# Score and maxima banks regrouped in the self and cross attention steps of a three-attention transformer block

## What is computed

```python
def _attn(x, ctx, wq, wk, wv, wo, bo, heads):       # heads = 20, dh = 16
    q, k, v = (x @ wq), (ctx @ wk), (ctx @ wv)      # split into heads
    sim = jnp.einsum('bhid,bhjd->bhij', q, k) * scale
    a = jax.nn.softmax(sim, axis=-1)
    out = jnp.einsum('bhij,bhjd->bhid', a, v)
    return out @ wo + bo
x = _attn(h1, h1, q1, k1, v1, o1_w, o1_b, heads) + x          # self, 512 keys
x = _attn(h2, context, q2, k2, v2, o2_w, o2_b, heads) + x     # cross, 1024 keys
```

## Time and profile before

| | us |
|---|---|
| median of 3 runs | 851.36 |
| the profiled execution | 850.15 |
| its span in the profile | 848.4 |
| self steps with maxima | 343.33 to 435.08 |
| self tail | to 448.7 |
| cross lead | 482 to 497 |
| first cross values | 501.64 |
| cross steps with maxima | to 690.7 |
| cross tail | to 713.1 |

### The profile page before, as it was taken

How to read it: one execution, slowest core, us unless ns; L and a number is a source line. 1 busy time by engine, 2 the same in 40 slices (tenths; PEclk the granted TensorE clock), 3 DMA queues, 4 the chain that set the end, 5 groups by cost and what they waited for, 6 DMA issues and landing times.

```text
span 848.4 us, 11644 instructions
## 1 busy us (share of the span) xinstructions
PE 802.2 (95%) x4178; PEld 442.8 (52%) x4178; DVE 584.4 (69%) x1102; ACT 488.7 (58%) x748; POOL 127.5 (15%) x209
## 2 busy tenths in 40 slices
PE   4889999999999999999999889999999999999998
PEld 3777644444466675333335543333333333678888
DVE  4354668777584648899956579999999962693241
ACT  4543544445553552776777767767677678862130
POOL 5000103100005241100014500000000002640000
PEclk9998999999999999999999969999999999999999
DMA  8887577532302066222135502232222120200000
GB/s 288 272 272 216 166 221 250 161 100 64 112 19 71 3 216 189 77 76 76 40 61 90 190 12 57 58 57 54 45 50 62 39 73 40 78 1 1 32 0 32
DMA packets 31255, 83.18 MB, mean 98 GB/s; under 512 B 5205, under 2 KB 9245, under 8 KB 28639
## 3 DMA queue, kind: packets, MB, share of 16 engines
q1 hardware_dynamic: 30398, 79.71, 32.6%
q0 software_dynamic: 800, 2.73, 1.0%
HBM read 56.12 MB, written 25.89 MB: 97 GB/s over the span
## 4 chain that ended last, share of the span: by engine, by line
PE 70%; DVE 15%; DMA 6%; ACT 4%; issue 4%; SPq 1%; POOL 0%; ACTq 0%; DVEq 0%; POOLq 0%
PE PS L1016 20%; PE PS L959 15%; PE PS L633 8%; PE PS L996 7%; PE PS L1647 7%; DVE maxp L1163 5%; PE PS L1665 4%; DMA k_d<-split 3%; DVE negm L1163 3%; PE PS L1468 3%; ACT probs L1123 2%; DVE turned L1208 1%; DMA w_v<-in_Wv 1%; ACT act_t L1541 1%; DMA q_sl<-msplit 1%
## 5 line engine op out<-in xcount | busy, mean ns | idle before, releaser
L1123 ACT ACTIVATE probs<-PS 128x1024 f32<-128x1024 f32 (+1 forms) x336 | 310.6, 972 | 138.4 <-PE PS L996 135.4
L1163 DVE TENSOR_REDUCE maxp<-PS 128x1 f32<-128x512 f32 (+1 forms) x400 | 251.7, 679 | 41.0 <-PE PS L959 40.0
L959 PE MATMUL PS<-k_sl,q_sl 48*128 48x512 f32 (+2 forms) x592 | 221.2, 446 | 8.7 <-DVE maxp L1163 2.1
L996 PE MATMUL PS<-q_sl,k_sl 50*128 50x512 f32 (+3 forms) x672 | 201.1, 428 | 4.2 <-ACT probs L1123 2.7
L959 PEld LDWEIGHTS PS<-k_sl,q_sl 48*128 48x128 f32 (+2 forms) x592 | 101.1, 186 | 163.5 <-DVE maxp L1163 105.3
L1163 DVE TENSOR_REDUCE negm<-PS 128x1 f32<-128x512 f32 (+1 forms) x192 | 121.6, 678 | 20.9 <-PE PS L959 20.1
L996 PEld LDWEIGHTS PS<-q_sl,k_sl 50*128 50x128 f32 (+2 forms) x672 | 101.3, 189 | 49.4 <-ACT probs L1123 21.1
L1016 PE MATMUL PS<-probs,v2c 128*32 128x512 f32 x640 | 87.4, 616 | 1.0
L675 DVE TENSOR_TENSOR split<-PS,split 128x512 fp32r<-128x512 f32 (+3 forms) x54 | 34.8, 649 | 52.4 <-ACT split L650 52.1
L1016 PE MATMUL PS<-probs,v0c 128*64 128x512 f32 (+1 forms) x256 | 62.0, 605 | 0.0
L650 ACT CAST split<-PS 128x512 fp32r<-128x512 f32 (+3 forms) x54 | 29.9, 555 | 50.2 <-PE PS L633 32.4
(11 more groups left out here) (203 smaller groups left out, 1092.9 us busy)
## 6 DMA issues: line engine op xcount, KB each, us to landing
k_d<-split SPq DMA_DIRECT2D x20, 512.0 KB, 3.9
q_d<-split SPq DMA_DIRECT2D x12, 512.0 KB, 4.0
k_sl<-k_d SPq DMA_DIRECT2D x8, 640.0 KB
k_sl<-k_d SPq DMA_DIRECT2D x40, 128.0 KB, 5.6
q_sl<-q_d SPq DMA_DIRECT2D x40, 128.0 KB
k_sl<-k_d SPq DMA_DIRECT2D x20, 256.0 KB, 5.4
w_raw<-in_ff_w SPq DMA_DIRECT2D x3, 1280.0 KB, 6.9
k_sl<-k_d SPq DMA_DIRECT2D x8, 320.0 KB
```

The lines of the kernel that those rows point to most:

```text
L959: nc.tensor.matmul(PS[0:a.qt, SBANKS[k % 3], 0:cn], q_view(g)[f:f + a.rows, j // a.stack, q * a.qt:(q + 1) * a.qt], k_view(g)[f:f + a.rows ...
L996: mm = nc.tensor.matmul(PS[0:sz, 2 * (x % 2) + half, 0:a.nq], k_view(g)[f:f + a.rows + 2, j // a.stack, t * 128:t * 128 + sz], q_view(g)[f ...
L1123: nc.scalar.activation(probs[0:a.size[t], x % PRING, :, 0:a.nq], PS[0:a.size[t], 2 * (x % 2):2 * (x % 2) + 2, 0:a.nq], ACT.Exp, scale=a.sc ...
L1163: nc.vector.tensor_reduce((maxp if nch > 1 else negm)[0:a.qt, g.turn, o:o + 1], PS[0:a.qt, SBANKS[k % 3], 0:a.chunks[c][1]], AX.X, ALU.max ...
```

## The change

In the self and cross streams (`st.single`) scores use single banks: 0, 1 and 2 in turn, and each head has an exponential of its own, 128 x 512, with a count of its own (`st.exp` starts at 3, `st.pair` counts scores). Bank 3 joins 4, 5 and 6 for the items and flips of the steps, the least recently used first. In the tails, from two steps after the last maxima (`st.tail`), scores may use banks 3 to 6 also, less the one that the last flip has. `bank_uses` and `score_banks` write down for each use its bank and the use before it. TensorE's order in a step becomes two items, two scores, two items, two scores, the values, the flips. The filler products go from 4 and 2 to 3 and 2. The first stream keeps pairs and three maxima banks. SyncE's waits on `st.pair` count scores in place of pairs (`scored_to`).

```diff
+def bank_uses(st):
+    st.bank, st.before = {}, {}
+    last, order = {}, [3] + list(SBANKS)
+    def take(ring, k, by):
+        b = next(n for n in order if n in ring)
+        st.bank[k], st.before[k], last[b] = b, last.get(b), by
+        order.remove(b)
+        order.append(b)
...
+        ring = (3,) + SBANKS if st.single and c >= st.lead else SBANKS
...
+def score_banks(st):
+    st.sbank, st.sbefore, last = {}, {}, {}
+    order = [0, 1, 2] + [b for b in (3,) + SBANKS if b != st.bank[st.flip_use[len(st.groups) - 1]]]
+    st.tail = len(st.steps) - st.lead + 2
+    for y in range(2 * st.all_pairs):
+        b = next(n for n in order if n < 3 or y >= 4 * st.tail)
+        st.sbank[y], st.sbefore[y], last[b] = b, last.get(b), y
+        order.remove(b)
+        order.append(b)
...
+        def score(i, t, j):
...
+            y = 2 * st.first_pair[i] + t * a.g + j
+            if st.sbefore[y] is not None:
+                pe.wait_ge(st.exp, 3 + st.sbefore[y] + 1)
+            elif y >= 3:
+                pe.wait_ge(st.score_free, st.all_items)
+            f = a.base(j)
+            nc.tensor.matmul(PS[:, st.sbank[y], 0:a.nq], ...).then_inc(st.pair, 1)
...
-            pe.wait_ge(st.exp, x + 3)
+            pe.wait_ge(st.exp, 2 * x + 5 if st.single else x + 3)
...
             for s in range(len(st.steps)):
-                if st is S_SELF and s == 0:
-                    keep_busy(4)
-                if s + 1 < len(st.steps):
-                    scores(*st.steps[s + 1], 0)
-                maxima(st.chunks_at(s), 0, 2)
+                more = s + 1 < len(st.steps)
                 if st is S_SELF and s == 0:
                     keep_busy(2)
-                if s + 1 < len(st.steps):
-                    scores(*st.steps[s + 1], 1)
+                maxima(st.chunks_at(s), 0, 1)
+                maxima(st.chunks_at(s), 1, 2)
+                if more:
+                    score(*st.steps[s + 1], 0)
+                if more:
+                    score(*st.steps[s + 1], 1)
                 maxima(st.chunks_at(s), 2, 3)
+                maxima(st.chunks_at(s), 3, 4)
+                if more:
+                    score(*st.steps[s + 1], 2)
+                if more:
+                    score(*st.steps[s + 1], 3)
                 for p in range(2):
                     values(*st.steps[s], p)
-                maxima(st.chunks_at(s), 3)
                 flips(st.chunks_at(s))
...
                 act.wait_ge(st.used, x + 1)
+                if st.single:
+                    for half in range(2):
+                        act.wait_ge(st.pair, 2 * x + half + 1)
+                        nc.scalar.activation(probs[:, x % PRING, half, 0:a.nq], PS[:, st.sbank[2 * x + half], 0:a.nq],
+                                             ACT.Exp, scale=a.scale).then_inc(st.exp, 1)
+                    x += 1
+                    continue
```

More of the change, by code:

```diff
@@ L97, in __init__ @@
         self.name = name
+        self.single = name != "first"
         self.groups = []
@@ L121, in __init__ @@
             self.negated_to.append(negated)
-        self.all_pairs = pairs
+        self.all_pairs, self.all_items = pairs, items
         self.lead = self.groups[0].a.lead
@@ L127, in pairs_to, with scored_to @@
         return self.first_pair[i] + self.groups[i].a.kt * self.groups[i].a.pairs
+    def scored_to(self, i):
+        return self.pairs_to(i) * (2 if self.single else 1)
     def chunks_at(self, s):
@@ L147 @@
 S_CROSS = Stream("cross", (A_CROSS,), 26)
+def bank_uses(st):
[6 more added lines that the diff above has]
+        order.append(b)
+    for c in range(len(st.steps) + 1):
+        ended, items = st.chunk(c)
+        if st is S_CROSS and c < st.lead:
+            for u in (2 * c, 2 * c + 1):
+                last[SBANKS[u % 3]] = ("item", 2 * (u + 1))
+            continue
+        ring = (3,) + SBANKS if st.single and c >= st.lead else SBANKS
+        for i, m in items:
+            take(ring, st.item_use[i, m], ("item", st.item_at[i, m] + 1))
+        if ended is not None:
+            take(ring, st.flip_use[ended], ("flip", ended + 1))
+def score_banks(st):
[7 more added lines that the diff above has]
+        order.append(b)
+for s in (S_FIRST, S_SELF, S_CROSS):
+    bank_uses(s)
+for s in (S_SELF, S_CROSS):
+    score_banks(s)
 def build(nc, ins, out_dram):
@@ L831, in sp_first @@
                 sp_load_m(sp, st, nm + 1)
-            sp.wait_ge(st.pair, st.pairs_to(i))
+            sp.wait_ge(st.pair, st.scored_to(i))
             if i + SLOTS < nm:
@@ L868, in sp_cross @@
         for i in range(SLOTS):
-            sp.wait_ge(before.pair, before.pairs_to(len(before.groups) - SLOTS + i))
+            sp.wait_ge(before.pair, before.scored_to(len(before.groups) - SLOTS + i))
             sp_load_k(sp, st.groups[i])
@@ L909, in flip_bank @@
             return OBANK
-        return SBANKS[st.flip_use[i] % 3]
+        return st.bank[st.flip_use[i]]
     def pe_attention(pe, st, side=None):
@@ L944, in bank_free @@
         def bank_free(k):
-            if k >= 3:
-                by, n = st.freed_by[k - 3]
+            if st.before[k] is not None:
+                by, n = st.before[k]
                 pe.wait_ge(st.score_free if by == "item" else st.flipped, n)
@@ L958, in item @@
             f = a.base(j)
-            nc.tensor.matmul(PS[0:a.qt, SBANKS[k % 3], 0:cn],
+            nc.tensor.matmul(PS[0:a.qt, st.bank[k], 0:cn],
                              q_view(g)[f:f + a.rows, j // a.stack, q * a.qt:(q + 1) * a.qt],
@@ L999, in scores @@
             mm.then_inc(st.pair, 1)
+        def score(i, t, j):
+            g = st.groups[i]
+            a = g.a
+            if t == 0 and j == 0:
+                pe.wait_ge(g.m_sem, g.m_loads)
+            y = 2 * st.first_pair[i] + t * a.g + j
[4 more added lines that the diff above has]
+            f = a.base(j)
+            nc.tensor.matmul(PS[:, st.sbank[y], 0:a.nq],
+                             k_view(g)[f:f + a.rows + 2, j // a.stack, t * 128:t * 128 + 128],
+                             q_view(g)[f:f + a.rows + 2, j // a.stack, :], start=True, stop=True).then_inc(st.pair, 1)
         def values(i, t, p):
@@ L1052, in pe_attention @@
             for p in range(st.groups[0].a.pairs):
-                scores(*st.steps[s], p)
+                if one:
+                    scores(*st.steps[s], p)
+                else:
+                    score(*st.steps[s], 2 * p)
+                    if st is S_SELF and p:
+                        keep_busy(3)
+                    score(*st.steps[s], 2 * p + 1)
         if one:
@@ L1771, in _ @@
             for st in (S_FIRST, S_SELF, S_CROSS):
-                act.sem_inc(st.exp, 2)
+                act.sem_inc(st.exp, 3 if st.single else 2)
             act.wait_ge(loaded_a, ALL_A)
```

7 lines of the change are left out of this document (3 added, 4 removed).

## The result

The changed kernel takes 865.22 us (median of 4 runs, 860.22 to 868.53) against 851.12 (4 runs of the kernel before); the ratio of the two is 1.012, with a 95% interval of 1.006 to 1.017 (the medians alone give 1.017). The interval lies above 1, so the kernel is slower, but by less than the 2% that a measurement of this kernel tells surely. The forecast was 865.0. The profiled execution took 864.16, 14.0 more than the one before (850.15).

A forecast was written before the change was run, and what follows sets the result against it. Bound by a latency ring through three maxima banks (2.70 us a step), not one engine; a 2.89 score ring replaces it. Terms sum to +13.5 on 850.15, 863.7; forecast 865.0 us, 1.6% slower, 852 to 876 for 8 in 10.

The forecast's parts named there:

- plain step: Steady self and cross steps: 2.89 us each, against 2.70 before.
- 65 cross steps: Cross steady stretch: 65 steps of 2.89 plus 8 flips of 0.22, 189.6 us against 181.05, +8.6.
- 32 self steps: Self steady stretch: 31 steps of 2.89, 8 flips and a last step of 2.66, 94.0 us against 91.75, +2.3.
- first tail step of cross: Start of the cross tail, one step without maxima ahead of the score: 2.66 us for 1.89, +0.8.
- rest of the tails: Remaining 7 and 11 tail steps, ScalarE nearly solid: 2.0 to 2.1 us a step, +0.5.
- two cross steps at the lower clock: First two cross steps at clock 0.50: the first 4.45 us for 4.16, the second some 0.5 more; +0.8 for both.
- starts: Two stream starts: fourth score waits for the first exponential, values for the ring, one filler product less in self; +0.5.
- the ring: Steady steps, six links: values, two maxima products, score to exponential, exponential, release, lone fourth score; 2.89 us against 2.70.
- the old ring: Steady steps before: a latency ring closed by three maxima banks, the values inside it; 2.70 us, gone with four banks.
- the first (VectorE's pace): Steady steps: new ring doesn't bind, step falls to VectorE's pace; -21.4 us, 830; chance 0.07.
- The second (the clock stays low): After the cross lead TensorE's clock stays low, steps 4.45 instead of 2.89; ten more give 881 us; chance 0.09.
- The third (dearer hand-overs): Steady steps: hand-overs cost more than their rows, such as two semaphores per exponential; 3.05 a step, 880 us; chance 0.06.

The follow-up runs named there:

- a score ahead: Changed kernel with the two first scores of a step ahead of all four maxima products; 844.19 us, ratio 0.987 to the kernel before.
- the late score: Changed kernel with the fourth score moved from ahead of the values to behind them in steady steps; 836.93 us (6 runs), ratio 0.980 to the kernel before.
- the doubling: Changed kernel with the first, or the second, pair of maxima products of each steady step issued twice; 889.53 and 860.09 us.
- the filler on VectorE: Changed kernel with one more useless 256-column reduction on VectorE after the fourth of each steady step; 865.88 us.
- the order alone: Kernel before with only the product order changed: two maxima products, two scores, two maxima products, two scores, values; 904.11 us, run again 889.21 (ratio 1.040).
- split values: Changed kernel with the first pair's values moved between second score and third maxima product, in steady steps but a group's first; 900.6 us, ratio 1.052.

## Why the prediction was right

Term by term, from the two profiled executions:

| term | predicted | measured |
|---|---|---|
| plain step | 2.89 | 2.90 |
| 65 cross steps | +8.6 | 190.25 - 181.05 = +9.2 |
| 32 self steps | +2.3 | 94.33 - 91.75 = +2.6 |
| first tail step of cross | +0.8 | 2.67 - 1.89 = +0.8 |
| rest of the tails | +0.5 | 14.70 - 14.66 + 22.55 - 23.02 = -0.4 |
| two cross steps at the lower clock | +0.8 | 4.55 + 4.26 - 8.03 = +0.8 |
| starts | +0.5 | +1.1 |
| sum | +13.5 | +14.1, of 14.0 |

The step that decided it, that the fourth score waits for the exponential of the first one of its own step, with the values queued behind it, held in every way in which it was tried: the idling stands where it was placed, work put on the ring lengthens the step by its own length and off the ring by nothing, and three ways of moving a link (a score ahead, a score behind the values, a semaphore off the path) change the step by what the link is worth; only the late score's step came 0.06 under what was expected, by its one link of 0.53. All six links measured within 0.01 us of the values taken. The exponential of 512 columns, the one link that no row of before showed, came at 0.60, as the Relu's row had it.

The first half of the reasoning held too: with four maxima banks the old ring is gone, maxima products idle for nothing, and the transposes no longer lengthen cross steps. A group's long steps in self are now 3.11, the flip's 0.22 over 2.90.

What was off was small. The tails got 0.4 shorter where I charged 0.5, nearly all of it in cross. Single exponentials start 0.49 apart (24 in 11.86 us), 0.98 for two. The pairs of before started 1.00 apart in the cross tail (20 in 19.99 us); the 0.92 that the prediction took from the earlier trace rows is that of the self tail, where ScalarE idled 0.24 in every other step. The steps gave 0.9 more than their terms: 2.90 for 2.89. VectorE idles 19.8 us in 65 steps, 0.30 each, where I said some 0.4; that holds for the plain steps, and the group work takes its share.

Two of the signs came out otherwise than foretold. TensorE idles 0.28 at the waiting score, not some 0.4. The weight loads of maxima products still wait for VectorE, 53 times and 42.0 us, though no matmul is late by it. And with the 612 ns that it estimates beside its own 0.60, the ring comes to 2.90, not to the 2.91 written there.

Of the +1.1 at the starts, 0.5 is there when the first stream ends (its last values start at 262.69 instead of 262.19), which the change leaves alone; the other 0.6, from there to the first self values (81.71 us for 81.14), is what the term was for. That the median lies 0.2 from the forecast is luck: the four executions spread over 8 us, and the sum can be held only against the profiled one, 864.16 for 863.7.

Of the rivals, the first (VectorE's pace) fell to the doubling and to the filler on VectorE. The second (the clock stays low) did not happen to this kernel: the clock was back after 13.65 us, as before. But it isn't fanciful: it happened in two executions, for 109 us each, when the order alone was changed. The third (dearer hand-overs) had a grain of truth in the wrong direction: the second semaphore was already inside the 0.49 that I had read from the earlier trace rows.

## To carry to other kernels

Where every engine is busy and none is full, write down for each buffer which instruction must end before its next writer may start, and what stands between the two on the in-order engine; the longest closed way round is the step, as in the kernels here but for the one with split values, whose step is TensorE's own work. A bank moved from one user to another closes a new ring: here three score banks for four scores put one wait inside the step, and the block of values, which nobody shortens, inside the ring. Then the cure is order, not speed: with the same instructions and banks, moving one score behind the values took the kernel from 865 to 837 us, a ratio of 0.980 (0.970 to 0.990) to the one before.

## What the runs showed that I had not expected

- Values of two heads took 0.98 us and of four heads 1.00: here the second two heads, side by side with the first two on the array's columns, cost 0.02, and splitting the block nearly doubled it (1.96).
- Of two waits ahead of a ScalarE instruction, the one listed last became an event of its own, 17 ns long and 0.06 us on the path. Listing the late-ending wait first took 0.06 us from the link and 0.06 from every step.
- TensorE's granted clock fell to 0.50 during or at the end of the cross lead in every profile. It came back after 10 to 24 us in most, and after 109 us in two executions of one order of products, although the records show TensorE busy in all of the 95.7 us of the window from 509.30 to 605.00. Seven of the fourteen profiles have another such stretch, of 3 to 14 us, where the self steps begin; the profiles of the kernels before and after have none there. What keeps it down wasn't found.
